# A shorter edge sort, a fourth x buffer, two loads moved and more pairs at the joint in a fused graph-and-attention kernel

## What is computed

```python
xn = layernorm(x)
h = relu(xn @ W1 + b1) @ W2 + b2
gnn = h + segment_sum(h[dst], src)              # segments are the rows src
k, q, v = split((layernorm(xn) * n1_g + n1_b) @ kqv_w + kqv_b)
kp, qp = exp(k @ w.T - |k|^2/2), exp(q @ w.T - |q|^2/2)
y = v + (qp @ (v.T @ kp).T) / (qp @ sum(kp)) @ proj_w + proj_b
mix = y + gelu((layernorm(y) * n2_g + n2_b) @ mlp_w1 + mlp_b1) @ mlp_w2 + mlp_b2
x1 = x + gnn + mix
out = x1 + ffn(layernorm(x1))                   # Haar transform, two small layers, inverse
```

## Time and profile before

| | us |
|---|---|
| median of 3 executions | 1723.69 |
| lowest, highest | 1717.75, 1730.77 |
| the profiled execution | 1722.76 |
| its span, first to last instruction | 1720.9 |

### The profile page before, as it was taken

How to read it: one execution, slowest core, us unless ns; L and a number is a source line. 1 busy time by engine, 2 the same in 40 slices (tenths; PEclk the granted TensorE clock), 3 DMA queues, 4 the chain that set the end, 5 groups by cost and what they waited for, 6 DMA issues and landing times.

```text
span 1720.9 us, 27109 instructions
## 1 busy us (share of the span) xinstructions
PE 1535.3 (89%) x8983; PEld 1269.8 (74%) x8983; DVE 1152.4 (67%) x2550; ACT 821.4 (48%) x1896; POOL 996.6 (58%) x1057
## 2 busy tenths in 40 slices
PE   5999999998888899999999977998898897788996
PEld 3778877777657788888888866876777786466664
DVE  6899999998344566756665663655554563478786
ACT  2234444444364444444544474665566462355552
POOL 3024444333677766767777777777777774556610
PEclk9999999999999999999999998999999998799998
DMA  6023232322335655556556566555555553566642
GB/s 198 13 68 119 90 93 84 102 75 90 111 104 157 196 164 165 171 174 205 179 173 185 170 193 203 194 189 189 187 190 190 185 181 119 171 204 206 200 164 76
DMA packets 88683, 263.65 MB, mean 153 GB/s; under 512 B 18555, under 2 KB 20603, under 8 KB 88546
## 3 DMA queue, kind: packets, MB, share of 16 engines
q1 hardware_dynamic: 47490, 149.05, 25.5%
q0 software_dynamic: 41056, 112.88, 23.0%
HBM read 210.64 MB, written 44.90 MB: 148 GB/s over the span
## 4 chain that ended last, share of the span: by engine, by line
PE 36%; DMA 27%; DVE 19%; ACT 7%; issue 6%; POOL 3%; SPq 1%; DVEq 1%; POOLq 0%; ACTq 0%
DMA z_rows<-sb_step 7%; DMA sb_step<-x 7%; DVE sb_weights L1573 6%; DMA sb_step<-sb_acc 4%; DMA sb_step<-x_t 3%; ACT sb_weights L1381 3%; PE bank L996 3%; PE bank L998 3%; PE bank L997 3%; DMA z_rows<-sb_weights 2%; DMA sb_weights<-x 2%; PE bank L788 1%; PE bank L790 1%; PE bank L789 1%; PE bank L1035 1%
## 5 line engine op out<-in xcount | busy, mean ns | idle before, releaser
L683 POOL DMA_INDIRECT sb_weights<-hidden_rows,sb_weights x830 | 825.2, 994 | 343.2 <-issue 220.0
L1381 ACT ACTIVATE sb_weights<-sb_const,sb_weights 128x125 f16<-128x125 f16 x880 | 266.1, 388 | 39.5 <-PE turn_bank L949 39.5
L1880 DVE TENSOR_TENSOR sb_acc<-sb_acc,bank 125x257 f32 x220 | 92.8, 422 | 191.1 <-PE bank L949 172.2
L1573 DVE TENSOR_TENSOR sb_weights<-sb_weights 128x512 f32<-128x512 f32 (+3 forms) x256 | 164.4, 684 | 3.6
L1880 DVE TENSOR_TENSOR sb_acc<-sb_acc,turn_bank 125x257 f32 x220 | 92.4, 420 | 109.0 <-PE turn_bank L949 99.6
L650 POOL TENSOR_SCALAR sb_const<-sb_const 125x2 f32<-125x2 f32 x25 | 9.6, 385 | 239.2 <-ACT sb_step L1283 239.2
L1299 ACT ACTIVATE sb_step<-sb_step 125x256 f32<-125x256 f32 x100 | 48.0, 503 | 202.6 <-DVE sb_step L1746 201.8
L788 PE MATMUL bank<-sb_w_parts,sb_x_high 128*125 128x512 f32 (+1 forms) x400 | 139.3, 348 | 0.0
L790 PE MATMUL bank<-sb_w_parts,sb_x_low 128*125 128x512 f32 (+1 forms) x400 | 135.2, 338 | 0.0
L789 PE MATMUL bank<-sb_w_parts,sb_x_high 128*125 128x512 f32 (+1 forms) x400 | 135.0, 337 | 0.0
L1385 ACT ACTIVATE sb_weights<-sb_weights,sb_const 128x1000 f16<-128x1000 f16 x110 | 124.2, 1129 | 3.6
(11 more groups left out here) (374 smaller groups left out, 4366.7 us busy)
## 6 DMA issues: line engine op xcount, KB each, us to landing
sb_step<-x SPq DMA_DIRECT2D x55, 500.0 KB
sb_step<-x_t SPq DMA_DIRECT2D x50, 500.0 KB, 6.9
sb_weights<-hidden_rows,sb_weights POOLq DMA_INDIRECT x830, 4.4
y_rows<-sb_step SPq DMA_DIRECT2D x25, 500.0 KB
sb_weights<-x SPq DMA_DIRECT2D x20, 500.0 KB
sb_step<-y_rows SPq DMA_DIRECT2D x17, 500.0 KB
z_rows<-sb_step SPq DMA_DIRECT2D x17, 500.0 KB
sb_step<-z_rows SPq DMA_DIRECT2D x13, 504.0 KB
```

The costliest lines, as they stand in the source:

```text
L683: pool.indirect_dma_start(out=ring[:, r % RING * 2 + h, 0:HID], out_offset=None, in_=table, in_offset=bass.IndirectOffsetOnAxis(ap=row_of[ ...
L1381: mm = act.activation(hit[q % 2][:, i, :], iota_h[:, :], ACT.Abs, bias=less_lane[:, q * BP + i // 2, i % 2:i % 2 + 1])
L1573: sort_op(dve.tensor_tensor(half(target, c, lo), a, b, op))
L1880: dve.tensor_tensor(dst, dst, (BE, BH)[n % 2][0:P, 0:RW], ALU.add).then_inc(g_add, 1)
```

## The change

Four edits. **The sort** stops at blocks of 256 keys: the last level keeps only its bits 16 to 8, which takes away eight of 153 stages, one of them a turned one. The keys stay where the last transpose puts them, in `turn_bank`, and `rank_part(22)` takes the last key of each block as a maximum. The copy of half of the turned keys moves from DVE to ACT (`lower_keys`), which waits for the transposes and does it ahead of `exps` or ahead of `q_kept`; the stages of turns 17 to 21 are dealt anew, and `rank_part(22)` and `rank_part(23)` move from the end of turn 21 and the middle of turn 22 to the middle of turns 21 and 22. **The mlp turns** get a fourth x buffer, in the place where `interp` lies until turn 2, and SP loads x two turns ahead: it waits for the store of z(a-2) first, loads x(a+2), and then does the rest. **Two loads** (y(2) and mlp2_w) move from the first place behind stage two to its turn 23, behind a wait for the last product that uses their place. **The joint** does twelve pairs instead of six; the last turns do 46 instead of 52.

```diff
-SORT = [(level, bit) for level in range(1, 18) for bit in reversed(range(level))]
+SORT = [(level, bit) for level in range(1, 18) for bit in reversed(range(level)) if level < 17 or bit >= 8]
...
-    return sum((4 if bit == level - 1 and level < 17 else 2) + turned(k) for k, (level, bit) in enumerate(SORT[:i]))
+    return sum(4 if bit == level - 1 and level < 17 else 2 for level, bit in SORT[:i])
...
 SORT_DEAL = ((15, 1), (5, 3), (2, 6), (3, 3), (2, 3), (6, 1), (4, 0), (7, 0), (3, 2), (5, 2), (5, 1),
-             (2, 5), (4, 3), (2, 3), (2, 3), (3, 2), (2, 5), (9, 0), (3, 4), (1, 4), (3, 2), (3, 4))
+             (2, 5), (4, 3), (2, 3), (2, 3), (3, 2), (2, 5), (6, 0), (3, 3), (4, 3), (6, 0), (0, 0))
...
-TURNED_LATE = (6, 11, 12, 13, 15, 16, 17, 19, 20, 21)
+TURNED_LATE = (19,)
...
+def turned_part(part):
+
+    if part < len(SORT_PARTS) and SORT_PARTS[part][0] < SORT_PARTS[part][1] and turned(SORT_PARTS[part][0]):
+        return SORT_PARTS[part][0]
+
+
+def turns_before(i):
+
+    return sum(turned(k) for k in range(i))
...
-TURN, SECOND, BETWEEN, MLP, JOIN, TAIL_TURN = (6, 14, 16), [14, 10, 9, 8] + [7] * (STEPS - 4), 4, [10] + [6] * (STEPS - 1), 6, 2
+TURN, SECOND, BETWEEN, MLP, JOIN, TAIL_TURN = (6, 14, 16), [14, 10, 9, 8] + [7] * (STEPS - 4), 4, [10] + [6] * (STEPS - 1), 12, 2
...
-        z3 = [x3[:, 0], x3[:, 1], z_first[2]]
+        z3 = [x3[:, 0], x3[:, 1], z_first[2], z_first[0]]
...
+                    sp.wait_ge(w_mm, 4 * STEPS + 1)
+                    load_yd(2)
+                    sp.dma_start(mlp2_w, chunks(d["L0_mix_mlp_w2"])).then_inc(w2m_in, 16)
...
-                sp.dma_start(z3[u % 3][0:P], x_d[:, 2 * u:2 * u + 2, :]).then_inc(x3_ld[u % 3], 16)
+                sp.dma_start(z3[u % 4][0:P], x_d[:, 2 * u:2 * u + 2, :]).then_inc(x3_ld[u % 4], 16)
...
-                sp.dma_start(z_d[1:P + 1, t.u * 2:t.u * 2 + 2, :], z3[t.u % 3][0:P]).then_inc(z_st[t.u % 3], 16)
+                sp.dma_start(z_d[1:P + 1, t.u * 2:t.u * 2 + 2, :], z3[t.u % 4][0:P]).then_inc(z_st[t.u % 4], 16)
...
-                sp.wait_ge(z_st[t.u % 3], 16 * (t.u // 3 + 1) + 1)
+                sp.wait_ge(z_st[t.u % 4], 16 * (t.u // 4 + 1) + 1)
...
             def late_io(a):
+                if 2 <= a and a + 2 < STEPS:
+                    z_stored(steps[a - 2])
+                    load_xd(a + 2)
                 if a + 3 < STEPS:
                     sp.wait_ge(zadd, a + 2)
                     sp.wait_ge(h_rows, a + 2)
                     load_yd(a + 3)
-                if 2 <= a and a + 1 < STEPS:
-                    z_stored(steps[a - 2])
-                    load_xd(a + 1)
+                if a == TAIL_TURN:
+                    sp.wait_ge(ev("pe_fc1"), 1)
+                    load_xd(3)
...
@@ -577,8 +607,6 @@
             sp.wait_ge(v_mm, STEPS + 1)
             load_yd(1)
             load_xd(0)
-            sp.dma_start(mlp2_w, chunks(d["L0_mix_mlp_w2"])).then_inc(w2m_in, 16)
-            load_yd(2)
             load_xd(1)
             load_xd(2)
             store_y(Step(2, STEPS - 1))
...
-            for t in steps[-3:]:
+            for t in steps[-4:]:
                 z_stored(t)
...
+                if part == 2 * (SORTED - 1):
+                    turn_keys(len(SORT))
...
+            def lower_keys(part):
+
+                i = turned_part(part)
+                if i is not None:
+                    act.wait_ge(sort_tr, turns_before(i) + 2)
+                    act.copy(span_half(keys[i % 2], 0, low_span(i)), span_half(turn_bank[:, :], 0, low_span(i))).then_inc(keys_ok, 1)
...
                     high_parts(next_step(t), w_mm, t.u * 2)
                 act.wait_ge(scaled, t.u + 2)
+                lower_keys(2 * t.u)
                 if t.u == STEPS - 1:
                     r_rows(t)
                 exps(t, lambda t: act.wait_ge(kadd, t.u + 1))
...
                 if 0 < t.u < STEPS - 1:
                     stats(next_step(t))
+                lower_keys(2 * t.u + 1)
                 q_kept(t.u)
...
-            hits_until(BEFORE_LAST - JOIN)
+            hits_until(BEFORE_LAST - JOIN + spread(JOIN, 3)[0])
             for u in range(3):
                 copy_degrees(steps[u])
-                if u == 1:
-                    hits_until(BEFORE_LAST)
+                if u < 2:
+                    hits_until(BEFORE_LAST - (spread(JOIN, 3)[2], 0)[u])
...
                 if turned(i):
-                    dve.wait_ge(sort_tr, (level - 10) * 2 + (bit == 6) + 2)
+                    dve.wait_ge(sort_tr, turns_before(i) + 2)
+                    dve.wait_ge(keys_ok, turns_before(i) + 2)
                     b_at = turn_bank[:, :]
-                    sort_op(dve.tensor_copy(half(a_at, 0, lo), half(b_at, 0, lo)))
-                    dve.wait_ge(sort_ok, sort_n[0] + 1)
...
-            sorted_keys = keys[len(SORT) % 2]
+            sorted_keys = turn_bank[:, :]
...
                 if u == SORTED:
-                    dve.wait_ge(sort_ok, sort_n[0] + 1)
-                    last_keys = sorted_keys.bitcast(I32).rearrange("p (q c) -> p q c", c=256)[:, :, 255]
-                    ts(last_bits, last_keys, SRC_BITS + 7, ALU.logical_shift_right)
+                    dve.wait_ge(sort_tr, turns_before(len(SORT)) + 2)
+                    seq(dve.tensor_reduce(last_keys, sorted_keys.rearrange("p (q c) -> p q c", c=256), AXIS.X, ALU.max))
+                    ts(last_bits, last_keys.bitcast(I32), SRC_BITS + 7, ALU.logical_shift_right)
...
                 sort_part(2 * t.u)
-                if t.u == SORTED:
-                    rank_part(SORTED + 1)
+                if t.u in (SORTED - 1, SORTED):
+                    rank_part(t.u + 1)
                 dve.wait_ge(ex, t.g * 2 + 3)
                 dve.wait_ge(kadd, t.u + 1)
                 dve.tensor_tensor(kps[0:P], kps[0:P], kp[0:P], ALU.add).then_inc(kadd, 1)
                 sort_part(2 * t.u + 1)
                 q_and_v(t.u)
-                if SORTED <= t.u + 1 < STEPS:
-                    rank_part((SORTED, SORTED + 2, SORTED + 3)[t.u + 1 - SORTED])
+                if SORTED <= t.u < STEPS - 1:
```

More of the change, by code:

```diff
@@ L8 @@
                               mybir.dt.int32)
-ALU, ACT = mybir.AluOpType, mybir.ActivationFunctionType
+ALU, ACT, AXIS = mybir.AluOpType, mybir.ActivationFunctionType, mybir.AxisListType
 N, D, E = 6250, 512, 100000
@@ L76, with low_span, span_half @@
 SORT_PARTS = sort_schedule()
+def turned_part(part):
[3 more added lines that the diff above has]
+    return sum(turned(k) for k in range(i))
+def low_span(i):
+    level, bit = SORT[i]
+    across = level >= 10 and bit >= 7
+    return 2 ** bit if not across else 2 ** (bit - 10) if bit >= 10 else 128 * 2 ** (bit - 7)
+def span_half(v, c, lo):
+    return v.rearrange("p (h c l) -> p h c l", c=2, l=lo)[:, :, c]
 def spread(count, parts):
     return [count * (i + 1) // parts - count * i // parts for i in range(parts)]
-TURN, SECOND, BETWEEN, MLP, JOIN, TAIL_TURN = (6, 14, 16), [14, 10, 9, 8] + [7] * (STEPS - 4), 4, [10] + [6] * (STEPS - 1), 6, 2
+TURN, SECOND, BETWEEN, MLP, JOIN, TAIL_TURN = (6, 14, 16), [14, 10, 9, 8] + [7] * (STEPS - 4), 4, [10] + [6] * (STEPS - 1), 12, 2
 BEFORE_SECOND = [sum(TURN) + sum(SECOND[:u]) for u in range(STEPS + 1)]
@@ L260, in build_program @@
         keys = [edge(COLS), edge(COLS)]
-        last_bits, last_tile = edge(4, dt=I32), edge(4)
+        last_bits, last_tile, last_keys = edge(4, dt=I32), edge(4), edge(4)
         within, in_last, iota_p = edge(4, NT, dt=F16), edge(4, NT, dt=F16), edge(P)
@@ L389, in build_program @@
         x_ld, x2_ld, xt_ld = (pair(n) for n in ("x_in", "x2_in", "xT_in"))
-        x3_ld, y_ld, z_st = ([sem(f"{n}{k}") for k in range(3)] for n in ("x3_in", "y_in", "z_stored"))
+        y_ld = [sem(f"y_in{k}") for k in range(3)]
+        x3_ld, z_st = ([sem(f"{n}{k}") for k in range(4)] for n in ("x3_in", "z_stored"))
         acc_ld = pair("sums_in")
@@ L838, in turn_for @@
             def turn_for(part):
-                if part < len(SORT_PARTS) and SORT_PARTS[part][0] < SORT_PARTS[part][1] and turned(SORT_PARTS[part][0]):
-                    turn_keys(SORT_PARTS[part][0])
+                if part == 2 * (SORTED - 1):
+                    turn_keys(len(SORT))
+                elif turned_part(part) is not None:
+                    turn_keys(turned_part(part))
             def sort_part(u):
@@ L1563, in sort_op @@
                 inst.then_inc(sort_ok, 1)
-            def half(v, c, lo):
-                return v.rearrange("p (h c l) -> p h c l", c=2, l=lo)[:, :, c]
+            half = span_half
             def exchange(lo, a_at, b_at, target):
@@ L1592, in sort_stage @@
                 level, bit = SORT[i]
-                across = level >= 10 and bit >= 7
-                lo = 2 ** bit if not across else 2 ** (bit - 10) if bit >= 10 else 128 * 2 ** (bit - 7)
+                lo = low_span(i)
                 dve.wait_ge(sort_ok, sort_n[0] + 1)
@@ L1858, in _ @@
                 q_and_v(t.u)
-                if SORTED <= t.u + 1 < STEPS:
```

(7 more changed lines are left out.)

2 lines of the change are left out of this document (1 added, 1 removed).

## The result

The changed kernel takes 1756.08 us, median of four runs (1750.88 to 1758.97), the kernel before 1725.05 beside it: a ratio of 1.0158, interval 1.012 to 1.0196. The forecast was 1753, slower. The profiled execution has a span of 1756.5 us, 35.6 more than before, so its times add up to a little more than the medians' 31.

The account below looks back on a forecast made before the run. SP's DMA queue, full with three 5.5 us transfers a turn, was taken to bound the mlp turns. +45 - 9 - 5 - 5 - 7 + 11 = +30 on 1722.8 gave 1753 us, own range 1735 to 1774, 8 in 10 1712 to 1774.

Parts of the forecast that it names:

- The mlp turns: z(0) to z(20): SP's queue empties at each landing of z, so a turn takes 18.55 us; +45 us.
- the empty queue: Mlp turns: issuing into an empty queue costs 2.55 us a turn, 3.4 at the most.
- thinner gathers: Mlp turns: gathers share the DMA engines and are thinner in a longer turn; 0.5 us off, 19.05 to 18.55.
- The sort: Stage one: DVE has 19 us less work, but the row-scale loop limits the gain; -7 us, bounds -19 and +4.
- The two loads: Start of the mlp turns: y(2) and mlp2_w fill an idle queue earlier; -5 us, bounds 0 and -9.5.
- z(20) to z(24): End of the mlp turns: x of turn 24 earlier -9, `fetch_sums(0)` not behind x(24) -5, joint's one-hot batch +4; -10 us.
- the +4 of the joint: Joint[0] needs the one-hot batch ahead of the last mlp product, whose z store the first z loads wait for; 0 to 5.
- The joint: POOL issues 24 DMAs between roots(0) and roots(1), +12; batch +4; six pairs fewer in the last turns -5; sum +11 us.
- (1): Mlp turns: queue is not the bound, prefetch pays, POOL sets a turn of 15.9 us; 1707 us, chance 0.09.
- (3): Mlp turns: the empty queue costs little, 17.3 us a turn; 1728 us, chance 0.08.
- (4): Mlp turns: the change of order does nothing, since z(a-1) is late anyway; 1713 us, chance 0.04.
- Rival (2): Mlp turns: queue has room, the ring's lead lasts and PE sets a turn of 14.8 us; 1684 us, chance 0.07.

Follow-up runs that it names:

- e4_order_alone: Kernel before, three x buffers, with only late_io reordered: wait for z(a-2) and load of x(a+1) ahead of the y load; 1762.0 us, ratio 1.0172.
- e2_split: Changed kernel with every y and x load and z store of the mlp turns issued as two DMAs of 120 and 5 partitions; 1693.23 us, ratio 0.9791.
- e1_y_first: Changed kernel with late_io loading y(a+3) ahead of the wait for the store of z(a-2), four x buffers kept; 1735.79 us, ratio 1.0043.
- e5_sort_alone: Kernel before with only the sort edit; mlp turns, loads and joint as before; on another chip, 1842.33 us, ratio 0.9925.
- e6_loads_alone: Kernel before with only y(2) and mlp2_w loaded in turn 23 of stage two; on another chip, 1857.39 us, ratio 1.0012.
- e7_join_alone: Kernel before with only twelve pairs at the joint instead of six and the changed kernel's one-hot batches; on another chip, 1883.41 us, ratio 1.0137.
- e3_pool_joint: Changed kernel with one more POOL line, issuing the gathers of the 12 units behind the joint ahead of roots(0); 1751.13 us, ratio 1.0134.
- e10_before_split: Kernel before with y and x loads and z stores of the mlp turns in 120 and 5 partitions; on a third chip, 1871.15 us, ratio 0.9979.

## Why the prediction was right, and where it was not

**The mlp turns.** Right in mechanism and nearly in size: z(0) to z(20) +41.0 for +45, a turn of 18.40 us (z(2) to z(20)) for 18.55. e4_order_alone shows that the order alone does it, and e2_split that the queue's pace does. The two terms in it were mis-sized in opposite directions. By the semaphore events of the trace x, issued into the empty queue, lands after 7.2 us on average from z(2) to z(20): 1.7 for the empty queue at 5.5 a transfer, not 2.55; y and z follow at 5.6 each, where the forecast had 5.3. 2.55 was read from the end of the kernel, from one transfer. The 0.5 us taken off for thinner gathers did not come: with 27.1 MB of gathers for 28.5 between 1105 and 1403 us, a transfer took no less than before.

**That the same turn with y first would take 16.5.** This step of the working held for the kernel before only. e1_y_first gave 17.4, with transfers of 5.8 us, and the cause of that is open.

**The sort.** Forecast -7, measured -11.6 on the page and 13 us in e5_sort_alone. The step that failed is that six turns of 15.4 us, limited by DVE, would lose only 0.35 each. DVE's first instructions show turns 5 to 16 taking 172.0 us before and 164.1 after: turns 7, 12 and 16 fell from 15.4 or 15.5 to 13.7 or 13.8. Turns 0 to 4 together take 2.9 more, most of it in turn 4, so the +2 for these seventeen turns was -4.9. The waits of the changed kernel between 100 and 422 us:

```profile
ACT sb_weights L1385 <- PE turn_bank L863: 62.7, 12, 6.1
DVE sb_step L1789 <- POOL sb_const L683: 18.6, 12, 4.3
...
DVE sb_weights L1624 <- ACT sb_weights L1385: 5.4, 2, 2.7
...
DVE sb_weights L1616 <- ACT sb_weights L1385: 2.1, 1, 2.1
...
DVE sb_weights L1610 <- ACT sb_weights L1385: 1.4, 1, 1.4
```

ACT does wait for PE's transposes, as foreseen, 62.7 us in all, but that was idle time; DVE waits for the copy only four times, 8.9 us in all. What I had right are the redealt turns: turn 17 -4.8 (for -4), 18 -0.6 (-1), 19 +2.8 (+3), 21 -7.0 (-7). Turn 22, where the rank parts moved, costs 2.4 that I had left out. (16 x 0.65 is 10.4, not 10.6, which changes nothing.)

**Stage two.** +7.1 where I had 0. On the page 2.4 of it is turn 22, at a granted clock of 0.92 instead of 1.00 and one us more of idle PE. e5_sort_alone keeps all of its 12 us in its total, so I take the rest for what one profiled execution happens to show, which is not settled. From turn 24 of stage one to this store the four profiles of the first chip with the new sort take 569.4 to 571.7 us, the two with the old sort 562.3 and (e4_order_alone) 567.0: part of it may belong to the change there.

**The two loads.** -8.6 on the page, inside the bounds of 0 to -9.5; ACT waits 8.14 us for y(3) instead of 16.55. e6_loads_alone shows nothing, on a chip with another bound, so the cause is argued from the page and not shown.

**z(20) to z(24).** -4.8 for -10. `skip_rows(24)` starts 10.8 us after z(20) landed, 22.5 before: -11.7 for -9. From there to z(24) it takes 6.9 us more, where I had 1 less (-5 and +4), and both terms of that failed. The first is `fetch_sums(0)`: I had PE's wait of 6.0 us go away. It stayed.

```profile
PE bank L1148 <- DMA sb_step<-sb_acc: 5.8, 1, 5.8
```

It no longer queues behind x(24) alone, but behind x(24) and z(22), which went out together at 1431.35 and 1431.65, as the drained queue makes them. The second is the +4 of the joint. From the end of the first two pairs of joint[0] to z(24) it was 12.5 us before (1450.04 to 1462.54) and is 19.0 now (1466.61 to 1485.62), +6.5. PE's wait for the one-hot batch, before in joint[1], behind the last mlp product, and then changed, in joint[0]:

```profile
1453.32 0.33 PE L946 MATMUL bank<-sb_weights 128*125 128x257 f16 x1 [0.48 <-ACT sb_weights L1385]
```

```profile
1469.87 0.33 PE L976 MATMUL bank<-sb_weights 128*125 128x257 f16 x1 [3.26 <-ACT sb_weights L1424]
```

The wait is 3.3 us, and the forecast had put nothing for two things that come with it: two more pairs ahead of the last mlp product, 1.1 us, and that product itself. It took 3.04 us before, at a granted clock of 1.00, and takes 4.56 now, at 0.63, right behind PE's idle time. e7_join_alone shows the same: +6.2, the product 4.59 us at 0.63, in e6_loads_alone 3.02 at 1.00.

**The joint.** +14.8 for +12 between the roots, and -2.2 for -5 in the last turns: POOL's 24 gathers are the cause (30.7 us between the roots in e7_join_alone against 15.7). That I called this DVE's loss alone was too simple: with POOL's queue cleared in e3_pool_joint only 9.7 us came back on the page, as the sums' load was late next.

**The rivals.** (1), (3) and (4) are refuted by 18.4 us a turn. Rival (1), that POOL sets the pace, is what e2_split reached, once its condition (a transfer under 4.5 us) was made true, but at 15.4 us a turn and not at 15.9. The 15.9 was misread: POOL's 246.4 us of work and 61.9 between gathers are 308 of 330 us, not 318, so twelve gathers are 15.3. Rival (2), PE setting the pace at 14.8, did not come about even there; POOL was full before PE.

**The total.** That it came within 3 us owes something to luck. Misses of -4.6 (sort), -3.6 (loads) and -4.0 (mlp turns) stood against +7.1, +5.2, +2.8 and +2.8 (stage two, z(20) to z(24), the roots, the last turns).

## What to carry over

Where a chain alternates store, load, store at a steady beat, count the transfers between two landings before adding a buffer: three of 5.5 us in a turn of 16.5 meant a full queue, and then a wait put ahead of the issues empties the queue and costs its refill in every turn. Look at the partition count of each large DMA: issued into an empty queue, 500 KB of 125 partitions took 7.2 us in one DMA, with y and z right behind it, and by the same events 5.2 on average as 120 and 5, by itself. And weigh a wait that you take away only against what is late next, here the sums' load once POOL's gathers were out of the way.

## What the runs showed of the hardware

The mlp turns of the kernel before take 16.6 us on one chip and, in e5_sort_alone and e7_join_alone, which leave them as they were, 17.9 and 17.7 on another, with a mean turn of stage two of 22.1 us instead of 19.4 (e5_sort_alone, y stores of turns 3 to 22) and stage one the same to within a microsecond; on such chips PE waits between matmuls of one product, 19 of 250 us in e10_before_split, for nothing that the profile shows. A change that fits the bound of one chip can be worth nothing on the next: the split was 2.1% faster than before together with the changed kernel's other edits on the first, 0.2% alone on two others. The late semaphore events of a landing go with the partition count: five for 125 partitions, fourteen for 126, twenty for 120 and 5 in two DMAs. From an empty queue and with no gathers beside them, a store of 500 KB on 125 partitions took 6.2 us and a load of 504 KB on 126 took 3.8. And gathers slow what is beside them: five such loads took 18.1 us with them and 13.0 without.
